# The last token tile goes to expert slots like the others, instead of through all eight experts

## The reference, cut to what matters

```
h = layernorm(x) * (1 + ca) + sa
x = x + ga * attn(h)          # attn: a scan over the 512 positions (GRU and a state space, mixed)
h = layernorm(x) * (1 + cb) + sb
x = x + gb * ffn(h)           # ffn: 8 experts of 128 -> 512 -> 128, the best one for each token

def ffn(x):                   # x: 4096 tokens x 128
    probs = softmax(x @ gate_w.T);  idx = argmax(probs);  w = probs[idx]
    out = 0
    for e in range(8):
        ye = relu(x @ w1[e] + b1[e]) @ w2[e] + b2[e]
        out = out + where(idx == e, ye * w, 0)
```

## Time and profile before

| | us |
|---|---|
| median of 3 runs | 695.53 (695.49 to 697.72) |
| the profiled execution's own time | 697.02 |
| its span, first to last instruction | 695.17 (the page: 695.2) |
| PE busy / DVE busy / ACT busy / POOL busy | 684.6 / 533.8 / 429.5 / 121.0 |
| granted TensorE clock, mean | 0.999 |
| last operation of the scan (step 511) ends | 633.8 |
| last slot's result in `y_sb` ends | 679.65 |
| last PE work of the dense tile | about 691 |
| last DVE operation ends | 693.1 |

### The profile page before, as it was taken

How to read it: one execution, slowest core, us unless ns; L and a number is a source line. 1 busy time by engine, 2 the same in 40 slices (tenths; PEclk the granted TensorE clock), 3 DMA queues, 4 the chain that set the end, 5 groups by cost and what they waited for, 6 DMA issues and landing times.

```text
span 695.2 us, 35722 instructions
## 1 busy us (share of the span) xinstructions
PE 684.6 (98%) x13868; PEld 641.9 (92%) x13868; DVE 533.8 (77%) x3216; ACT 429.5 (62%) x2688; POOL 121.0 (17%) x209
## 2 busy tenths in 40 slices
PE   7999999999999999999999999999999999999997
PEld 5899999989999999999999999999999999998896
DVE  4777777777887777887887788878877888875666
ACT  4555555556666666557666775676666676666442
POOL 4011111111011111112112211121212212221202
PEclk9999999999999999999999999999999999999999
DMA  8916000603522100044322000642210163323431
GB/s 309 364 61 220 8 7 7 223 33 133 183 94 86 53 15 15 14 168 175 126 86 71 22 15 19 215 163 95 94 61 23 56 230 117 110 67 93 154 102 55
DMA packets 45658, 71.97 MB, mean 104 GB/s; under 512 B 6156, under 2 KB 28498, under 8 KB 45362
## 3 DMA queue, kind: packets, MB, share of 16 engines
q1 hardware_dynamic: 41490, 64.38, 26.3%
q0 software_dynamic: 1984, 4.07, 2.0%
q10 hardware_dynamic: 2016, 1.25, 0.6%
HBM read 14.31 MB, written 21.04 MB: 51 GB/s over the span
## 4 chain that ended last, share of the span: by engine, by line
PE 97%; DVE 1%; issue 0%; ACT 0%; DVEq 0%
PE rs_bank L1223 34%; PE nz_bank L1223 24%; PE hid_bank_b L1223 12%; PE work L1223 11%; PE y_bank L1223 9%; PE hid_bank_a L1223 7%; DVE fin_g L1199 0%; DVE acc L1157 0%; DVE o_sb L1204 0%; DVE hid_b L1179 0%; ACT xT L783 0%; ACT hid_a L790 0%; DVE prob L1023 0%; DVE y_sb L1193 0%; DVE fin_g L1211 0%
## 5 line engine op out<-in xcount | busy, mean ns | idle before, releaser
L1223 PE MATMUL nz_bank<-h_ring,wg 128*64 128x16 f32 x4088 | 207.2, 211 | 0.0
L798 ACT ACTIVATE r_fac<-rs_bank 128x8 f32<-128x8 f32 x512 | 91.6, 179 | 169.0 <-PE rs_bank L1223 161.8
L1223 PE MATMUL rs_bank<-s_ring,ws_sb 128*64 128x128 f32 x1024 | 195.1, 272 | 0.0
L1223 PEld LDWEIGHTS nz_bank<-h_ring,wg 128*64 128x64 f32 x4088 | 160.8, 136 | 1.4
L1223 PE MATMUL rs_bank<-mw,wg 128*64 128x8 f32 x2044 | 146.8, 202 | 0.0
L1223 PE MATMUL rs_bank<-u,wg 128*64 128x8 f32 x2044 | 140.6, 206 | 0.1
L1223 PEld LDWEIGHTS rs_bank<-s_ring,ws_sb 128*64 128x64 f32 x1024 | 127.2, 136 | 9.1
L1104 DVE TENSOR_TENSOR_SCAN nz_bank<-r_fac,nz_bank 128x16 f32<-128x16 f32 x512 | 99.7, 195 | 46.3 <-ACT r_fac L798 30.8
L1108 DVE SCALAR_TENSOR_TENSOR mw<-v_fac,h_ring 128x8 f32<-128x8 f32 x512 | 85.7, 167 | 57.5
L1223 PEld LDWEIGHTS rs_bank<-mw,wg 128*64 128x64 f32 x2044 | 103.4, 135 | 18.8 <-DVE mw L1108 4.6
L804 ACT ACTIVATE v_fac<-nz_bank 128x8 f32<-128x8 f32 x512 | 91.1, 178 | 42.0
(11 more groups left out here) (181 smaller groups left out, 1125.0 us busy)
## 6 DMA issues: line engine op xcount, KB each, us to landing
wx<-w_all SPq DMA_DIRECT2D x58, 578.0 KB, 3.5
rows<-zeros SPq DMA_DIRECT2D x3, 4096.0 KB, 14.5
rows<-y_sb SPq DMA_DIRECT2D x66, 64.0 KB, 1.8
w_all<-in_w SPq DMA_DIRECT2D x2, 2048.0 KB, 15.1
xs_sb<-rows SPq DMA_DIRECT2D x54, 64.0 KB, 2.9
x_sb<-in_x SPq DMA_DIRECT2D x1, 1920.0 KB, 7.4
out<-o_sb SPq DMA_DIRECT2D x19, 64.0 KB, 2.6
out<-o_sb ACTq DMA_DIRECT2D x13, 64.0 KB, 1.7
```

The source lines that it names most:

```text
L798: nc.scalar.activation(r_fac[:, k, :, 1], r_cols(q, t), ACT.Tanh, scale=0.5).then_inc(rn_ready, 1)
L1223: last = nc.tensor.matmul(out[c:c + COLS], weights[:, c:c + COLS], moving, start=start, stop=stop, skip_group_check=skip_group_check)
```

## The change

- SIZE becomes [6, 7, 7, 7, 5]: tile 26 joins the fourth group, the last group holds tiles 27 to 31. All 32 tiles go to slots; there are 67 slots.
- All of the dense tile goes: `ORDER`, `gate`, `acc`, `dense_y`, the eight rounds on PE, their relus, and the two last DVE operations.
- Tile 31's `post` part 3, its transposition and routing come one step later (`work_step`: from step 520 on, work of step t runs in t + 1), its rank products stay in step 526, its placing and its scatter come in step 527. `load_fixed` comes in step 528, `lay_out` of the last group in steps 535 to 539 (before: 525 to 529).
- The tiles of the last group but one are gathered and finished every 6 steps instead of 9.

By the planner's rules 430 of the 603 units now lie ahead of step 512 and 173 in the tail. Slots 47 to 54 of the fourth group fill the steps from 512 to 536, the last group's first X is in step 536, its last B+ in step 590, and its five gathers come behind that.

The core of the diff:

```diff
-SIZE = [6, 7, 7, 6, 5]
+SIZE = [6, 7, 7, 7, 5]
...
-ORDER = [("slot", n) for n in range(SLOT0[NG - 1])]
-for i in range(SIZE[-1] + E - 1):
-    ORDER.append(("slot", SLOT0[NG - 1] + i))
-    if i % 4 == 3 and i // 4 < 2:
-        ORDER.append(("expert", i // 4))
-ORDER += [("expert", e) for e in range(sum(what == "expert" for what, _ in ORDER), E)]
...
 def place_at(j, n):
+    if j == NT - 1:
+        return (j + 2) * T - 1
...
 def dispatch_at(k, n):
     at = (last_tile(k) + 2) * T
-    return at + (2 + n if at < NT * T else 13 + n // 2)
+    return at + (2 + n if at < NT * T else 7 + n // 2)
 def scatter_at(j):
+    if j == NT - 1:
+        return (j + 2) * T - 1
...
-                u = max(u, gather[FIRST[k] + i - 1] + (9 if k < NG - 1 else 3), NT * T + 13)
+                u = max(u, gather[FIRST[k] + i - 1] + (6 if k < NG - 1 else 3), NT * T + 13)
...
+        def work_step(c, t):
+            return t if c < NT or t < 8 else t - 1 if t > 8 else None
...
-                if u == scatter_at(NS - 1) + 1:
+                if u == scatter_at(NT - 1) + 1:
                     for n in range(FIXED0, EXTRA0):
                         load_fixed(n)
...
-                    if t == 8:
+                    if w == 8:
                         post(j, 3)
-                    if 10 <= t <= 15:
-                        route(j, 1 - q, t)
-                if c == NT and t == 13:
...
-                if c == NT + 1 and t < E:
-                    b2_e = w_all[:, t, 2 * FC * P + FC:W_EXP]
...
+                    if w and 10 <= w <= 15:
+                        route(j, 1 - q, w)
...
-                    if second and kind == "B" and i in EXPERT_OF:
-                        e = EXPERT_OF[i]
-                        ge(eng, w2_done, 2 * i + 2)
-                        ge(eng, acc_step, E + e)
-                        nc.vector.scalar_tensor_tensor(out=acc[:, :], in0=dense_y(e), scalar=gate[:, e:e + 1],
-                                                       in1=acc[:, :], op0=ALU.mult, op1=ALU.add).then_inc(acc_step, 1)
...
             steps(step)
-            j = NT - 1
-            ge(eng, acc_step, 2 * E)
-            ge(eng, o_ready, j)
-            nc.vector.tensor_tensor(fin_g[:, :], acc[:, :], mod_gb, ALU.mult).then_inc(fin_step, 1)
...
-                    if t == 14:
+                    if t == (13 if j == NT - 1 else 14):
                         ge(eng, onehot_ready, c)
```

More of the change, by code:

```diff
@@ L89 @@
 NBUF = 7
-ND = 4
 RING = 12
@@ L166, in order_of_units @@
 def order_of_units(k):
-    first, end = SLOT0[k], SLOT0[k + 1] if k < NG - 1 else len(ORDER)
+    first, end = SLOT0[k], SLOT0[k + 1]
     todo = [("X", first, 0)]
@@ L173, in order_of_units @@
             todo += [("B", n - 1, 0), ("B", n - 1, 1)]
-        if k == NG - 1 and n + 1 in SLOT_OF:
+        if k == NG - 1 and n + 1 < end:
             todo += [("X", n + 1, 0)]
@@ L289 @@
 UNITS, ON_ACT, RELU_OPEN = schedule()
-Y_STEP = {SLOT_OF[i]: u for u, what in UNITS.items() for kind, i, second in what
-          if kind == "B" and second and i in SLOT_OF}
+Y_STEP = {n: u for u, what in UNITS.items() for kind, n, second in what if kind == "B" and second}
 Y_AT = {u: n for n, u in Y_STEP.items()}
@@ L316 @@
 TAIL_X = TAIL + 1
-X_STEP = {SLOT_OF[i]: u for u, what in UNITS.items() for kind, i, second in what if kind == "X"}
+X_STEP = {n: u for u, what in UNITS.items() for kind, n, second in what if kind == "X"}
 U_END = max(max(FINAL_AT.values()), max(UNITS)) + 4
@@ L648, in step @@
                     load_expert(n)
-                for j in range(NS):
+                for j in range(NT):
                     if u == OUT_AT[j] + 3 and OUT_AT[j] < TAIL:
@@ L1164, in step @@
                     tables(t)
-                for i in range(NS):
+                for i in range(NT):
                     for n in range(PLACE_STEPS):
@@ L1174, in step @@
                     pre(tile, part)
-                for kind, i, second in UNITS.get(g, []):
-                    if second and kind in "AC" and (kind, i, second) not in ON_ACT:
+                for kind, n, second in UNITS.get(g, []):
+                    if second and kind in "AC" and (kind, n, second) not in ON_ACT:
                         h = kind == "C"
-                        ge(eng, w1b_ready, 2 * i + h + 1)
-                        nc.vector.tensor_scalar(hid_b[:, h, :], hid_bank[1][:, 0:P], bias1(i, 2 * h + 1), 0.0,
+                        ge(eng, w1b_ready, 2 * n + h + 1)
+                        nc.vector.tensor_scalar(hid_b[:, h, :], hid_bank[1][:, 0:P], bias1(n, 2 * h + 1), 0.0,
                                                 ALU.add, ALU.max).then_inc(relu_b_ready, 1)
-                    if second and kind == "B" and i in EXPERT_OF:
-                        e = EXPERT_OF[i]
-                        ge(eng, w2_done, 2 * i + 2)
-                        ge(eng, acc_step, E + e)
-                        nc.vector.scalar_tensor_tensor(out=acc[:, :], in0=dense_y(e), scalar=gate[:, e:e + 1],
-                                                       in1=acc[:, :], op0=ALU.mult, op1=ALU.add).then_inc(acc_step, 1)
-                    if second and kind == "B" and i in SLOT_OF:
-                        n = SLOT_OF[i]
-                        ge(eng, w2_done, 2 * i + 2)
+                    if second and kind == "B":
+                        ge(eng, w2_done, 2 * n + 2)
                         ge(eng, y_stored[n % NBUF], 16 * (n // NBUF))
@@ L1298, in hold_clock, with unit @@
                 mm(hid_bank[1][:, 0:width], ident, w_sb[:, W_MOD:W_MOD + width], start=True, stop=True)
-            def unit(kind, i, second):
+            def unit(kind, n, second):
                 h = kind in "CB"
                 at = (2 * h + second) * P
-                dense = i in EXPERT_OF
-                e, n = EXPERT_OF.get(i), SLOT_OF.get(i)
-                fixed = None if dense else fixed_expert(n)
-                b = None if dense or fixed is not None else turn(n) % NBUF
-                whole = dense or fixed is not None
-                e = e if dense else fixed
+                e, b = fixed_expert(n), None if fixed_expert(n) is not None else turn(n) % NBUF
                 if kind == "X":
@@ L1334, in unit @@
                 if kind == "D" and not second:
-                    if not dense:
-                        ge(eng, y_ready, n)
-                    elif e == 0:
-                        ge(eng, hs_ready, NT * T)
-                        ge(eng, h_ready, NT * T)
-                    elif e >= ND:
-                        ge(eng, acc_step, E + e - ND + 1)
-                ge(eng, (relu_a_ready, relu_b_ready)[second], 2 * i + h + 1)
-                last = mm(dense_y(e) if dense else y_bank[:, 0:P], (hid_a, hid_b)[second][:, h, :],
-                          w_all[:, e, FC * P + at:FC * P + at + P] if whole else wx2[:, b, at:at + P],
+                    ge(eng, y_ready, n)
+                ge(eng, (relu_a_ready, relu_b_ready)[second], 2 * n + h + 1)
+                last = mm(y_bank[:, 0:P], (hid_a, hid_b)[second][:, h, :],
+                          w_all[:, e, FC * P + at:FC * P + at + P] if b is None else wx2[:, b, at:at + P],
                           start=kind == "D" and not second, stop=kind == "B" and second > 0)
```

77 lines of the change are left out of this document (24 added, 53 removed).

## The result

The changed kernel took 697.80 us (median of 20 runs, 696.47 to 700.82), the kernel before 695.38 (20 runs, 694.76 to 697.72) beside it: ratio 1.0035 [1.0026, 1.0044], 2.4 us slower. The forecast was 694.4 in a range of 691.6 to 697.0: wrong in sign and outside the range.

A forecast was written before the change was run, and what follows sets the result against it. Scan steps bound the kernel to 633.8 us, then PE's unit list; the change trades list for bare DMA chains. X at 653.5, last result 680.8, plus 13.3 gives 694.1; 694.4 from the median, range 691.6 to 697.0.

The forecast's parts named there:

- The scan, "0": Steps 0 to 511: ten units fewer, filler instead, cost 0, within 0.3 us either way; step 511 ends at 633.8.
- Tile 31's placing: On DVE ahead of the last group: routing ends 647.45, placing takes 0.80 and ends 648.25; POOL's scatter 0.81 later.
- 18.2 predicted: PE's own list ahead of the last group's first X: two more slots of 2.08 each, PE ready at 652.0.
- "The load's landing 2.0", X at 653.5: Tile 31's rows: scatter lands in 2.3, SP's load in 2.0; first X at 653.5, 5.7 later than before.
- The third rival, the clock, at 0.03: PE's clock falls to 1.2 GHz while waiting for the first X; slots add 3.9, total 698.3; chance 0.03.
- The twelve slots, 27.3: Last group, first X to last result: 6.3 + 18.7 + 1.4 + 0.6 + 0.3, ending at 680.8.
- the 0.6 that I had put for the finishes: In the last group's slots: finishes of tiles 22, 24 and 26 push relus by 0.2 each, bounds 0 to 1.0.
- second rival: SP's eight loads delay stores and tile 20's gather; DVE's finish has 1.5 us in hand; total 698, chance 0.10.
- 25.0 forecast: Fourth group's first gather, tile 20: starts near 658.8 behind SP's stores, scan ending at 633.8; lands near 661.5.
- "From the last DVE operation's end to the end of the span 2.06.": At the program's end: 2.06 us from the last DVE operation, taken from the earlier profile.
- 13.3: Last result to span end: 2.73 + 5.0 + 2.7 + 0.77 + 2.06, bounds 12.6 and 14.3.

The follow-up runs named there:

- layout_late: Changed kernel with the fourth group's lay_out five steps later (455 to 464 instead of 450 to 459): 698.87 us, ratio 1.0028 to the kernel before.
- again: The changed kernel, unchanged, run once more for a second profile: 699.56 us, ratio 1.0034 to the kernel before.
- split: Changed kernel with three of the last group's eight fixed loads in step 528, five behind slot 54's store: 698.28 us, ratio 1.0032 to the kernel before.
- shift: Changed kernel with ten further small products on PE at the start, results unused: 698.22 us, ratio 1.0029 to the kernel before.
- fill4: Changed kernel with four unused products on PE ahead of the last group's first X: 698.95 us, ratio 1.0028 to the kernel before.
- nowait: Changed kernel whose first eight last-group loads read input x without waiting for tile 31's scatter (other results): 696.58 us, ratio 0.9990 to the kernel before.
- early_split: Changed kernel with tile 31's routing two steps earlier and five of the eight fixed loads behind slot 54's store: 694.58 us, ratio 0.9988 to the kernel before.
- early: Changed kernel with tile 31's routing, placing and scatter two steps sooner: 697.46 us, ratio 1.0006 to the kernel before.
- before_gather: Kernel before with one more gather, unread, behind POOL's last one: 697.92 us, ratio 1.0013 to the kernel before.
- early_split_shift: Changed kernel with tile 31's routing two steps earlier, five fixed loads behind slot 54's store, ten small PE products at the start: 695.47 us, ratio 0.9997.

## Why the prediction was wrong

**The scan, "0".** Failed, by some 0.4. The step rates of the earlier trace rows say that units cost the scan nothing, as far as a count of whole steps of 1.2 us in 40 us can tell; they don't say what `lay_out`, moved by 16 steps, meets on DVE. It met a finish in step 451 (row above), and layout_late took the loss away.

**Tile 31's placing.** Right: 14.64 us behind the scan for 14.42, scatter 0.83 behind it for 0.81. PE was ready 18.74 behind the scan in *again*, 0.5 later than the 18.2 predicted; since the rows came later still, that didn't count.

**"The load's landing 2.0", X at 653.5.** Failed: 2.80 and 3.20 in the two profiles of the changed kernel; in split and shift the load landed in 1.8 and 1.7, but the scatter took 4.25 and 4.04 for the 2.3 of the earlier trace rows. I took medians of DMAs spread over 65 us for one serial chain that PE waits for. The Trainium skill (DMA: Bandwidth & Descriptors, Anatomy of one DMA) gives a DMA a fixed 2.0 us, in a section on those that POOL issues; the loads here, which SP issues, took 1.7 to 2.0 where no q8 transfer fell on them and 2.8 to 4.2 where one did; POOL's scatter took 2.3 and, in split and shift, over 4.0. The Trainium skill (Runtime: NRT & Kernel Launch, Instruction fetch mechanics) calls the cost of crossing a 16 KiB boundary of the instructions mostly hidden; here the 0.9 to 1.6 us of such a transfer stand beside a DMA that is 1 to 2.4 us late.

**The third rival, the clock, at 0.03.** Mis-sized. PE's wait was 2.30 in the profile of the changed kernel and the granted clock fell to half for some 6 us: 29.01 instead of 27.25 from X to the last result, 1.8 us. In the profiles with such a wait it fell after 2.30, 2.54, 2.85 and 3.33 us and stayed after 0.96, 1.91 and 2.58. I had read a window with 1.09 us of idle time in all as the nearest row and didn't ask what a wait longer than forecast would do on top. By fill4 it is still not the main part of the median's loss.

**The twelve slots, 27.3.** Right as a number, in part by luck: 27.25 and 27.28 without a fall of the clock, each with a wait of 0.9 us on DVE that the sum doesn't have (tile 21's gather in *again*, a result buffer's store in nowait). early_split, without it, has 26.64; the 0.6 that I had put for the finishes didn't come. For the finish of tile 20 I had given DVE 1.5 us in hand (second rival, which the text ahead calls the first one), with a gather that lands in 2.7. In early and layout_late that gather took 4.3 us, in *again* the next one 5.79: this used them up, more than the loads on SP did, which let the first gather of *again* start 25.7 behind the scan's end for the 25.0 forecast. That SP's loads of weights beside them slow the gathers is not shown; that they start sooner in early_split covers it.

**"From the last DVE operation's end to the end of the span 2.06."** Failed: the chain took 14.05 instead of 13.3. The row was right for DVE's and the last store's tail, but it is not the only chain to the end. POOL's closing instruction ended 0.2 us ahead of SP's in the kernel before, so no row showed it as a wait; in the changed kernel it ends 1.1 us behind SP's and sets the end: 2.58 to the first gather, 5.0 for five of them, 6.48 behind the last.

The forecast was thus a gain of 1.1 us worked out as the difference of a list that got shorter and a chain that got longer, with each link of the chain at its typical length. Behind the scan's end the kernel before took 61.34 us and the forecast was 60.3; the two profiles of the changed kernel have 64.11 and 61.95. The scan's end itself differs by up to 1.5 us between executions of one kernel (633.25 and 634.78). The median is 3.4 us above the forecast: by subtraction some 0.4 for the scan, 0.75 for the end, and the rest for the late rows with what follows from them (clock, late gathers), in shares that change from one execution to the next. A gain from the dense rounds is at most small: early_split, with the chain two steps sooner, has 60.42 behind the scan's end, near the forecast, and its gain over the kernel before is 0 to 0.1%.

## To carry to other kernels

A long serial chain of DMAs that takes the place of engine work is as late as its unluckiest link, so give it slack or start it sooner; the medians of its links add up to little more than its best case. Before a wait is put on an engine that only issues DMAs, list what is queued behind it, here stores whose results another engine picks up 10 us later. And ask which engine's last instruction ends the program: a tie in the profile (here 0.2 us) hides the one that will bind next.

## What the runs showed of the hardware

- POOL's closing DRAIN ends 6.1 to 6.25 us behind the start of POOL's last indirect DMA in all profiles, whether its result is used or not; the span ends 0.2 to 0.4 us behind it, also where DVE has been done for 3.1 to 3.3 us (changed kernels, before_gather).
- A 16 KB transfer on q8 lies over 219 of the 262 of SP's DMA issues that took more than 0.65 us (all eighteen profiles, from 25 us on), and over 653 of the 3576 shorter ones. A first load of the chain on which one falls lands 1 to 2.4 us later (2.8 to 4.2 instead of 1.7 to 2.0), a scatter 1.7 to 1.9. Whether the transfer is the cause is open.
- Indirect gathers that are ready at the same time start 1.25 to 1.3 us apart in every profile. At the end of the program, with little beside them, they land 2.5 to 2.7 behind their start; in the middle of the tail, beside SP's weight loads, up to 6.0 (early_split_shift).
